# Turning the odd score tiles of a two-layer attention kernel on VectorE instead of TensorE

## The reference

```python
# layer 0: 16 heads of width 8
tp = (silu(time_emb) @ Wt + bt)[:, None, :]
shift_msa, scale_msa, gate_msa, shift_mlp, scale_mlp, gate_mlp = split(tp, 6)
h = layernorm(x, g1, be1) * (1 + scale_msa) + shift_msa
q, k, v = heads(h @ Wqkv + bqkv)
attn = softmax(einsum('blhd,bmhd->bhlm', q, k) * 8 ** -0.5)
x = x + gate_msa * (einsum('bhlm,bmhd->blhd', attn, v) @ Wproj + bproj)
h = layernorm(x, g2, be2) * (1 + scale_mlp) + shift_mlp
x = x + gate_mlp * (gelu(h @ W1 + b1) @ W2 + b2)
# layer 1: rmsnorm and film in place of layernorm, one head of width 128,
# the same order of attention and mlp, no gates
```

## Time and profile before

| | us |
|---|---|
| median of 3 runs (262.51 to 263.51) | 262.57 |
| time of the profiled execution | 263.23 |
| span of the profiled execution | 261.3 |
| attention 0, from the first `scores0` to the last `weigh0` | 19.2 to 104.8 |
| busy: TensorE 237.8, VectorE 168.8, GpSimd 151.2, ScalarE 148.8 | |

### The profile page before, as it was taken

How to read it: one execution, slowest core, us unless ns; L and a number is a source line. 1 busy time by engine, 2 the same in 40 slices (tenths; PEclk the granted TensorE clock), 3 DMA queues, 4 the chain that set the end, 5 groups by cost and what they waited for, 6 DMA issues and landing times.

```text
span 261.3 us, 10297 instructions
## 1 busy us (share of the span) xinstructions
PE 237.8 (91%) x3952; PEld 179.4 (69%) x3952; DVE 168.8 (65%) x509; ACT 148.8 (57%) x338; POOL 151.2 (58%) x161
## 2 busy tenths in 40 slices
PE   0588878998999998999999999889999999999995
PEld 0456565877778776677776669767776566777775
DVE  3868997889899998375445444688889445542002
ACT  2368566667768659925466655546557554444440
POOL 7442543855857768776666667786674555553110
PEclk9999999999999999999999999999999999999999
DMA  6964423333443552350000000000000011101112
GB/s 209 311 235 106 105 80 102 98 97 123 111 126 114 118 135 96 84 161 1 3 0 0 0 0 0 4 3 3 0 0 3 0 41 43 29 11 43 40 40 83
DMA packets 17451, 18.01 MB, mean 69 GB/s; under 512 B 2320, under 2 KB 13072, under 8 KB 17296
## 3 DMA queue, kind: packets, MB, share of 16 engines
q1 hardware_dynamic: 16848, 15.67, 20.8%
q10 hardware_dynamic: 576, 1.98, 2.3%
HBM read 11.48 MB, written 4.59 MB: 61 GB/s over the span
## 4 chain that ended last, share of the span: by engine, by line
PE 71%; DVE 11%; issue 5%; DMA 4%; SPq 4%; ACT 4%; POOL 1%; ACTq 0%; DVEq 0%; POOLq 0%
PE bank L1132 22%; PE bank L948 19%; PE bank L992 5%; PE bank L924 4%; PE bank L1022 4%; PE bank L1172 3%; PE bank L1043 2%; PE bank L1004 2%; ACT xhat L759 2%; DMA X<-x 2%; SPq L254 2%; DMA values_scratch<-Vs 2%; DVE St L579 2%; PE bank L1139 2%; PE bank L972 1%
## 5 line engine op out<-in xcount | busy, mean ns | idle before, releaser
L759 ACT ACTIVATE xhat<-X,shift,rstd 128x128 f32 (+1 forms) x96 | 40.2, 485 | 50.8 <-POOL shift L324 50.8
L1132 PE MATMUL bank<-W,Kx 128*128 128x128 f32 x512 | 59.6, 275 | 0.0
L1132 PEld LDWEIGHTS bank<-W,Kx 128*128 128x128 f32 x512 | 58.5, 192 | 1.0 <-issue 1.0
L948 PE MATMUL bank<-h,W 128*128 128x512 f32 x124 | 56.5, 595 | 0.1
L335 POOL TENSOR_TENSOR h<-hA,B 128x512 f32<-128x512 f32 x32 | 33.6, 1048 | 31.0 <-DVE hA L495 30.7
L814 ACT ACTIVATE Kx<-bank,col 128x512 f32<-128x512 f32 x64 | 39.2, 676 | 8.9 <-PE bank L948 8.9
L495 DVE TENSOR_TENSOR hA<-bank,A 128x512 f32<-128x512 f32 x32 | 21.7, 677 | 29.9 <-issue 15.0
L948 PEld LDWEIGHTS bank<-h,W 128*128 128x128 f32 x124 | 22.2, 190 | 21.8 <-issue 21.5
L343 POOL TENSOR_TENSOR Ss<-Sc,smax 128x512 f32<-128x512 f32 x16 | 16.8, 1050 | 26.6 <-DVE smax L521 26.3
L322 POOL TENSOR_TENSOR rstd<-v_sb,minus_half 128x4 f32<-128x4 f32 x24 | 24.6, 1025 | 11.8 <-DVE v_sb L480 6.7
L358 POOL TENSOR_TENSOR yG<-yG,gate 128x512 f32<-128x512 f32 x16 | 20.4, 1272 | 7.9 <-DVE yG L504 7.7
(11 more groups left out here) (124 smaller groups left out, 396.3 us busy)
## 6 DMA issues: line engine op xcount, KB each, us to landing
values_scratch<-Vs SPq DMA_DIRECT2D x8, 288.0 KB, 2.2
Vx<-values_scratch SPq DMA_DIRECT2D x32, 72.0 KB
gate<-gates_scratch SPq DMA_DIRECT2D x32, 64.0 KB, 2.1
gate<-gates_scratch SPq DMA_DIRECT2D x16, 128.0 KB, 2.7
out<-X SPq DMA_DIRECT2D x7, 256.0 KB, 2.3
Kx<-Ks SPq DMA_DIRECT2D x24, 64.0 KB, 1.9
W<-weights ACTq DMA_DIRECT2D x1, 1152.5 KB, 5.9
X<-x SPq DMA_DIRECT2D x4, 256.0 KB, 7.0
```

Source lines behind the costliest of these rows:

```text
L759: last = act.activation(xhat[:, p, P * t:P * (t + 1)], X[:, x_tile(gg, t), :], ACT.Identity, bias=shift[:, p, t:t + 1], scale=rstd[:, p, t ...
L948: last = pe.matmul(bank[2 + n][:, :], w(f"W1_{phase // 2}", n), h[:, p, :], start=True, stop=True)
L1132: last = pe.matmul(y[t // 2][:, P * t:P * (t + 1)], gT[:, p, n, P * t:P * (t + 1)], w(f"W2_{phase // 2}", n), start=(n == 0), stop=(n == N ...
```

## The change

Four things change, all of them in attention 0.

* `scores_T` goes. The odd tiles are turned by VectorE as well (`turn` with `odd` = 1), into a second half of `St` in SBUF. The two new calls stand after `row_stats` and after `update` in VectorE's queue, and one more in the preamble after `place_k(1)`.
* `modulate` of attention 0 leaves VectorE (its calls for the groups 2 to 9). ScalarE copies `hT_ps` to `hTs` (`move_hT`, behind `copy_scores` of (g,1) and ahead of `exps` of (g,0)), and GpSimd multiplies (`scale_hT`, behind `subtract_max` of (g,1) and ahead of `add_shift`).
* The heads of odd tiles come out in another order, so V and the projection get weights of their own for odd tiles (`Wv_odd`, `Wproj_odd`, 64 KB each). Both lie in the stretch of `W` that ScalarE's queue loads at the start.
* `weigh0` reads the odd tiles like the even ones.

```diff
-        Ss, St = sb("Ss", [P, 2, 2, GN]), sb("St", [P, GN])
+        Ss, St = sb("Ss", [P, 2, 2, GN]), sb("St", [P, 2, GN])
+        hTs = sb("hTs", [P, GN])
...
+            def scale_hT(gg, p, g):
+                pool.wait_ge(hTs_ready, g + 1)
+                pool.tensor_tensor(by_seq(hA[:, p, :]), by_seq(hTs[:, :]),
+                                   A[:, seqs(gg)].unsqueeze(2).broadcast_to([P, GB, L]), ALU.mult).then_inc(hA_ready, 1)
...
                 subtract_max(g, 1)
+                scale_hT(g + 2, p, g)
                 add_shift(g + 2, p, 0, g)
...
-            def turn(g, half):
+            def turn(g, half, odd):
                 hh = 2 * g + half
-                dve.wait_ge(s_shifted[0], hh + 1)
-                wait(dve, pt_ready[0], hh)
-                dve.transpose(St[:, :], Ss[:, half, 0, :]).then_inc(st_ready[0], 1)
+                dve.wait_ge(s_shifted[odd], hh + 1)
+                wait(dve, pt_ready[odd], hh)
+                dve.transpose(St[:, odd, :], Ss[:, half, odd, :]).then_inc(st_ready[odd], 1)
...
             place_k(1)
+            turn(0, 0, 1)
...
                 shift_scores(g, 1)
-                modulate(g + 2, p)
...
                 row_stats(g + 4)
+                turn(g, 1, 1)
                 normalise(g, p, 0)
...
+                if not last:
+                    turn(g + 1, 0, 1)
                 aggregate(g + 4, p, True)
...
+            def move_hT(gg):
+                act.wait_ge(hT_ready, gg + 1)
+                act.wait_ge(hA_ready, gg)
+                act.activation(hTs[:, :], hT_ps[:, :], ACT.Copy).then_inc(hTs_ready, 1)
...
-                for n, turned in enumerate((St, bank[7])):
+                for n in range(2):
...
                 copy_scores(g, 1)
+                move_hT(g + 2)
                 exps(g, 0)
...
-                    last = pe.matmul(to[:, t], h[:, p, P * t:P * (t + 1)], by_r if t % 2 else by_a, start=True, stop=True)
+                    last = pe.matmul(to[:, t], h[:, p, P * t:P * (t + 1)], of_odd if t % 2 else of_even, start=True, stop=True)
...
-                        from_ = P * (b % TB) + (rows_at(b, n) if odd(b) else L * n)
+                        from_ = P * (b % TB) + L * n
...
-                    last = pe.matmul(y_ps[:, P * t:P * (t + 1)], OTs[:, p, P * t:P * (t + 1)], w("Wproj"),
+                    last = pe.matmul(y_ps[:, P * t:P * (t + 1)], OTs[:, p, P * t:P * (t + 1)], w("Wproj_odd" if t % 2 else "Wproj"),
...
-                scores_T(g, 0)
...
-                scores_T(g, 1)
```

More of the change, by code:

```diff
@@ L39 @@
 SCALE1 = D ** -0.5
-W_NAMES = [("Wt", 6 * D), ("film1", 2 * D), ("film2", 2 * D), ("Wproj", D), ("v1", D), ("proj1", D),
-           ("Wqkv", 3 * D), ("W1_0", FF), ("W2_0", FF), ("q1T", D), ("k1T", D + 1), ("W1_1", FF), ("W2_1", FF)]
+W_NAMES = [("Wt", 6 * D), ("film1", 2 * D), ("film2", 2 * D), ("Wproj", D), ("Wproj_odd", D), ("v1", D), ("proj1", D),
+           ("Wqkv", 3 * D), ("Wv_odd", D), ("W1_0", FF), ("W2_0", FF), ("q1T", D), ("k1T", D + 1), ("W1_1", FF), ("W2_1", FF)]
 W_AT, W_ALL = {}, 0
@@ L141, in build @@
         rden_ready, o_used, ot_ready, ot_moved = (sem(n) for n in ("rden_ready", "o_used", "ot_ready", "ot_moved"))
-        qv1_ready, q1_moved, v1_moved, s1_ready, max1_ready, s1_used, p1_ready, den1_ready, rden1_ready, p1_scaled, pt1_ready, ssq_ready = (
-            sem(n) for n in ("qv1_ready", "q1_moved", "v1_moved", "s1_ready", "max1_ready", "s1_used", "p1_ready", "den1_ready",
+        hTs_ready, qv1_ready, q1_moved, v1_moved, s1_ready, max1_ready, s1_used, p1_ready, den1_ready, rden1_ready, p1_scaled, pt1_ready, ssq_ready = (
+            sem(n) for n in ("hTs_ready", "qv1_ready", "q1_moved", "v1_moved", "s1_ready", "max1_ready", "s1_used", "p1_ready", "den1_ready",
                              "rden1_ready", "p1_scaled", "pt1_ready", "ssq_ready"))
@@ L543, in shift_scores @@
                 row_max(g, half, 1)
-                turn(g, half)
+                turn(g, half, 0)
             def place_k(g):
@@ L800, in exps @@
                         wait(act, pv_done, hh)
-                    act.activation(PT[:, n, :], turned[:, :], ACT.Exp).then_inc(pt_ready[n], 1)
+                    act.activation(PT[:, n, :], St[:, n, :], ACT.Exp).then_inc(pt_ready[n], 1)
             def move_o(g, p):
@@ L968, in values0 @@
                 to = bank[2][:, :].rearrange("p (n t m f) -> p t n m f", n=HQ, t=TG, m=HQ)
-                by_r = w("Wqkv", 2).rearrange("p (r a f) -> p r a f", r=HQ, a=HQ)
-                by_a = w("Wqkv", 2).rearrange("p (r a f) -> p a r f", r=HQ, a=HQ)
+                of_even, of_odd = (v.rearrange("p (r a f) -> p a r f", r=HQ, a=HQ) for v in (w("Wqkv", 2), w("Wv_odd")))
                 for t in range(TG):
-                    last = pe.matmul(to[:, t], h[:, p, P * t:P * (t + 1)], by_r if t % 2 else by_a, start=True, stop=True)
+                    last = pe.matmul(to[:, t], h[:, p, P * t:P * (t + 1)], of_odd if t % 2 else of_even, start=True, stop=True)
                 last.then_inc(v0_ready, 1)
@@ L995, in scores0 @@
                 last.then_inc(s_ready, 1)
-            def scores_T(g, half):
-                hh = 2 * g + half
-                pe.wait_ge(s_shifted[1], hh + 1)
-                wait(pe, pt_ready[1], hh)
-                for n in range(GB // 4):
-                    at = slice(P * n, P * (n + 1))
-                    last = pe.transpose(bank[7][:, at], Ss[:, half, 1, at], ident[:, :])
-                last.then_inc(st_ready[1], 1)
             def weigh0(g, p, half, following=None):
@@ L1013, in weigh0 @@
                 even_o = bank[6][:, 0:OW].rearrange("p (a r f) -> p r a f", a=HQ, r=HQ)
-                odd_o = bank[6][:, OW:2 * OW].rearrange("p (a r f) -> p a r f", a=HQ, r=HQ)
+                odd_o = bank[6][:, OW:2 * OW].rearrange("p (a r f) -> p r a f", a=HQ, r=HQ)
                 for n in range(HQ):
@@ L1250 @@
     ws = {"Wt": L0_cond_Wt, "film1": L1_cond_film1_w, "film2": L1_cond_film2_w, "Wproj": L0_cond_Wproj,
-          "v1": L1_cond_v_w, "proj1": L1_cond_proj_w, "Wqkv": np.concatenate([heads(wqkv[:, 0], 0, 2, 1), heads(wqkv[:, 1], 0, 2, 1), heads(wqkv[:, 2], 1, 0, 2)], axis=1), "W1_0": L0_cond_W1,
+          "v1": L1_cond_v_w, "proj1": L1_cond_proj_w, "Wqkv": np.concatenate([heads(wqkv[:, 0], 0, 2, 1), heads(wqkv[:, 1], 0, 2, 1), heads(wqkv[:, 2], 1, 0, 2)], axis=1), "W1_0": L0_cond_W1, "Wv_odd": np.roll(heads(wqkv[:, 2], 1, 0, 2).reshape(D, HQ, HQ, HD), 2, axis=2).reshape(D, D), "Wproj_odd": np.roll(np.asarray(L0_cond_Wproj), D // 2, axis=0),
           "W2_0": chunks(np.asarray(L0_cond_W2)), "q1T": np.asarray(L1_cond_q_w).T, "k1T": np.concatenate([np.asarray(L1_cond_k_w).T, np.asarray(L1_cond_k_b)[:, None]], axis=1), "W1_1": L1_cond_mlp_w1,
```

## The result

The changed kernel took 269.57 us in the median of six executions (266.56 to 272.39), the kernel before 262.57 (261.6 to 266.02) beside it. Three of the six took 271.0 to 272.4 us and are left out of the ratio, which is 1.0156 with a 95% interval of 1.0103 to 1.0209. 262.57 x 1.0156 = 266.7 us, +4.1. The forecast of 265.2 (+2.6) had the sign, and its range of 263.2 to 267.6 holds the 266.7; the median over all six lies above it. The profiled execution took 268.18 us with a span of 266.4, against 261.3 before: +5.1.

The account below looks back on a forecast made before the run. VectorE was to replace TensorE as bound, at 10.15 us a group. Start +0.3, group 0 +1.3, groups 1 and 3 -0.4, groups 4 to 6 +1.4 gave +2.6: 265.2 us, range 263.2 to 267.6.

Parts of the forecast that it names:

- The floor of 8.5 us: TensorE, attention 0: without two `scores_T` a group its floor falls from 9.6 to about 8.5 us.
- the 1.5 us of idle a group: TensorE, groups 4 to 6: about 1.5 us idle a group, between `project0` and `keys0` or ahead of `scores0`.
- VectorE's queue: Attention 0: two turns of 0.63 more, one `modulate` of 0.57 less; 9.32 becomes 10.01 us a group, the new bound.
- the 0.14 for the wait: VectorE, half 0: the odd turn waits for GpSimd's subtraction and starts 0.14 us late, making 10.15 a group.
- the lower bound: GpSimd's new multiplication, priced like the addition of `B` at 1.05 us busy; the gate product's 1.28 was the upper bound.
- a ring at 10.0: Update, gate product, addition, `power`, subtraction, odd turn, back to `update`: 10.0 us round, nearly tying with VectorE.
- The second rival: Groups 2 to 6: near-tied waits on VectorE, GpSimd and the way from `h` add up; 267.2 us, chance 0.17.
- In middle groups TensorE's new slack hides it.: ScalarE's new copy, 0.50 us a group ahead of `exps` of (g,0), was to cost nothing in middle groups.
- Group 0: `power` of 3 starts 1.27 us later and TensorE waits through ScalarE, +1.3; VectorE's 1.3 runs in parallel.
- Start: 128 KB more in the weight load delay the first X tiles by 0.31 us at 424 GB/s; taken as +0.3.
- Groups 1 and 3: TensorE's savings may shorten them, between 0 and -1.18 us each; taken as -0.2 each, the waits there untouched.
- The saving goes through: Attention 0: turns cost VectorE under 0.42 us each, so groups hold or shrink; 258.7 us, chance 0.10.

Follow-up runs that it names:

- The ring shortened: Changed kernel with GpSimd's addition to X in attention 0 covering one row tile of four; 267.69 us, ratio 1.0106.
- the turns alone: Changed kernel with `modulate` back on VectorE, so the odd tiles are still turned by VectorE; 271.72 us, ratio 1.0293.
- VectorE relieved: Changed kernel with only the odd tiles of half 1 turned by VectorE, those of half 0 by TensorE again; 268.65 us, ratio 1.0219.
- The modulation alone: Kernel before with only the modulation moved to ScalarE and GpSimd, TensorE keeping its transposes and the old weights; 265.15 us, ratio 1.0075.
- both at once: Changed kernel with TensorE turning half 0's odd tiles and GpSimd's addition to X on one tile of four; 266.38 us, ratio 1.0102.
- the store held back: Changed kernel with the store of group 2's values held until the first half of group 2's scores is done; 268.81 us, ratio 1.0176.
- `power` earlier: Changed kernel with GpSimd's `power` of group 3 placed between `scale_hT` and `add_shift` in group 0; 268.46 us, ratio 1.0191.
- the later load: Changed kernel with the two odd weights in a transfer of their own, behind the others on ScalarE's queue; 267.54 us, ratio 1.0183.
- the weights alone: Kernel before with the two odd weights, 128 KB, added to its load and not used; 264.44 us, ratio 1.0061.

## Why the prediction was right, and where it was off

**TensorE's saving.** The transposes are gone and it bought nothing in the middle groups. The floor of 8.5 us was the sum of TensorE's own work; no group can come near it, because the loop over TensorE and ScalarE below is 9.9. Of the 1.5 us of idle a group that were forecast, 0.82 are in group 5 (9.84 - 9.02). Busy falls only from 9.52 to 9.02, since a wait of the weight loads hides in busy time: from `project0` to `keys0` are 88.34 - 87.17 = 1.17 us, before 0.90, and the loads of `keys0` wait there for GpSimd's `h`.

**VectorE's queue.** Right in kind and in size: a turn is 0.63, the queue 9.9 to 10.0. The ring shortened shows it as a bound at 10.01, the turns alone at 10.49. With the 0.14 for the wait, 10.15 was forecast and 10.08 measured: +1.17 for +1.4.

**GpSimd.** The price was at the lower bound, 1.05. The forecast had a ring at 10.0 and called it nearly tied. The number was good and the ring another: it was followed from `update` to the odd turn and back to `update` one group later, and that turn (86.22 in half 1) doesn't wait for GpSimd. The ring that the chain runs through goes on from `power` over the multiplication and `h` to the keys and the scores, and closes after two groups. With VectorE relieved it holds 10.05 by itself. The second rival had named this way; that both come to 10.0 is luck.

**ScalarE: the step that only just held.** "In middle groups TensorE's new slack hides it." There is little slack to hide it in. The loop of TensorE and ScalarE is 9.9 us long with the copy in it. The modulation alone, at 10.22, shows the price of the copy where nothing hides it, and both at once, at 9.92, that the slack which the change opened ended at 9.9 and not at TensorE's 8.5. In the changed kernel the copy costs nothing more, since the two others are at 10.0, so the forecast of 0 for it was right. Taking away one of the two gave nothing because of the other, and taking away both gave only 0.16 because of this third.

**Group 0.** +0.89 for +1.3, and the path was half wrong. `power` was later by 1.09 for 1.27. But the way over `power` had slack before: VectorE's folded rows ended group 0, at 13.08, and the way over `power` could have ended it 0.24 sooner. And VectorE's queue was counted as 1.3 longer and covered. Only two of the three new turns lie ahead of the folded rows, so it is 0.59 longer there, and it holds group 0 at 13.67 alone. The late `power` adds 0.29 on top. The forecast took VectorE's queue to cost nothing here.

**Start.** The mechanism was likely right (the load delays X), the place wrong: the second group of X, +0.86 for +0.3. The other 1.0 are slower first products, unforeseen and not explained.

**Groups 1 and 3.** Forecast -0.2 each, for TensorE's savings. Group 3 gave -0.80, but not by them: the wait of 1.04 us for the keys' transfer is gone, and against the 9.67 without it the group is 0.24 longer. Why the wait is gone isn't shown. Group 1 came to +1.56: one stall of 1.93 us where the earlier trace rows has 0.85 and 1.12, and after it `project0` and `keys0` at the lower clock, 2.08 + 1.76 us for 1.06 + 1.02. I had taken the stalls of the earlier trace rows as untouched by the change. Their number, length and consequence all vary from kernel to kernel and between executions; that is also why the six executions spread over 5.8 us where those before spread over 4.4.

**Last group.** -0.05 for 0, with the wait at `weigh0` 1.70 for 0.89 as the copy (0.47) and the missing transposes add up. The rest of the program gave +0.4, unforeseen.

**What was luck.** The forecast had +2.7 for group 0 and the groups 4 to 6 together, and they gave 2.06. The rest was forecast at -0.1 and gave +3.0, out of the start, group 1 and the end of the program. A range of 263.2 to 267.6 holds 266.7 because it was wide enough for that, not because these terms were in it. That the time rises was no luck: the groups 4 to 6 and group 0 are enough for it.

**The rivals.** "The waits add up" came nearest in number (267.2), but not by its mechanism: the middle groups were shorter than forecast, and the surplus is the start and group 1. "The saving goes through" is refuted by the 0.63 of a turn.

## What to carry to other kernels

Before moving work off the engine on the chain, add up the starts in the queue of the engine that receives it. Then follow each ring that crosses engines once round, and find out what ends a stretch today before pricing what will delay it. Here three bounds (VectorE's queue and two rings) lay within 0.15 us of each other, and relieving one alone (half of the turns back, the short addition) moved a group by 0.07 us at most. A copy placed ahead of the exponentials is paid in full as soon as the engine behind it has no slack. Stalls with no releaser in the first pass of a loop belong to the uncertainty of any prediction for a kernel with many small products: here they were worth up to 2.2 us each, and more when the clock fell after them.

## What the runs showed of the hardware

A stall of TensorE can be followed by the lower clock, and need not be. After 1.93 us the granted clock was 0.50 at 46 to 48 us in the changed kernel; after the same 1.93 us with the store held back it stayed at 1.00, and fell to 0.50 at 58 to 60 after one of 2.24. With `power` earlier it was 0.50 at 32 to 34 after a wait of only 1.35 us for VectorE, following shorter ones; after the same wait of 1.35 us at the same place it stayed at 1.00 with the store held back and with the later load. The Trainium skill, page "TensorE: Matmul & The Clock Gate", section "HAM oscillation — how this bites in real kernels", says that waits between stretches of work can put the clock back to its lower level; the traces agree with that for the waits of these rows after which it fell, and the first 1.93 with the store held back shows that not every wait of this size does it.

The first two 512-wide products took 1.02 us in some kernels and 1.91 in others, with a granted clock of 1.00 in the windows of both. A clock read from the windows is therefore no proof that the products ran at full speed; the duration of a known product is the better witness.

With 128 KB more in a load on one queue, a group of X on another landed later: its statistics start at 9.87 to 10.57 in the ten kernels with that load (10.48 with the weights alone), for 9.29 and 9.07 in the two without the added weights. At 424 GB/s the 128 KB would be worth 0.31.
